# A three-branch decoder layer on one core: the passage from the projections to the first expert, rearranged

## The reference

```
# 1: recurrent attention (8 heads of 64)
b = (q * k).sum(-1) * SCALE;  a = -softplus(x @ W_alpha.T + bias).sum(-1)
ln = logaddexp(a_t + ln, b_t)
nm, sg = log-magnitude and sign of  sg*exp(a_t + nm) + sign(v_t)*exp(b_t + log(|v_t| + EPS))
y_t = sum over heads of sg * exp(nm - ln);   attention = y @ W_o.T
# 2: eight experts, gated by token
h = relu(x @ proj_in[e].T);  o = h @ proj_out[e].T
gate[b, s, e] = sum over k of weights[b, k, s] * (ensembles[b, k, s] == e)
# 3: gated ternary feed-forward net, three layers of 1024
x = layernorm(x + branch)          # after each of the three
```

## Time and profile before

| | us |
|---|---|
| median of 3 executions | 833.45 (833.44 to 836.83) |
| the profiled execution | 834.23 |
| its span, first to last instruction | 832.4 |
| TensorE busy | 791.9 (95%) |
| VectorE busy | 460.7 (55%) |
| ScalarE busy | 308.4 (37%) |
| GpSimd busy | 99.2 (12%) |
| mean granted TensorE clock | 0.985 of 2.4 GHz |

### The profile page before, as it was taken

The page is one execution under the profiler, slowest core; times in us unless marked ns, Lnnn a source line. Parts: engine busy times, 40 slices in busy tenths (PEclk is TensorE's granted clock), DMA queues, the critical chain, the costliest instruction groups (busy, mean ns, idle before and its releaser), DMA issues.

```text
span 832.4 us, 12868 instructions
## 1 busy us (share of the span) xinstructions
PE 791.9 (95%) x4342; PEld 685.4 (82%) x4342; DVE 460.7 (55%) x1119; ACT 308.4 (37%) x552; POOL 99.2 (12%) x100
## 2 busy tenths in 40 slices
PE   5999849999999999999999989999999999999995
PEld 4888728888899998999899988888888888888884
DVE  4788657665577775777665655323632363245113
ACT  5677622222232313223232226342634354326331
POOL 2465520000220201102020000000000000000000
PEclk9999969999999999999999999999999999999998
DMA  8700000000311223131311000000000000000000
GB/s 265 254 0 2 0 2 2 0 2 26 102 51 41 90 57 94 51 101 38 95 46 51 26 10 1 1 0 1 25 0 0 0 25 0 0 7 19 1 1 26
DMA packets 16451, 31.46 MB, mean 38 GB/s; under 512 B 1680, under 2 KB 6160, under 8 KB 16400
## 3 DMA queue, kind: packets, MB, share of 16 engines
q1 hardware_dynamic: 16400, 30.82, 11.8%
HBM read 28.72 MB, written 2.10 MB: 37 GB/s over the span
## 4 chain that ended last, share of the span: by engine, by line
PE 44%; issue 44%; DVE 7%; ACT 2%; POOL 1%; DMA 1%; DVEq 0%; POOLq 0%; SPq 0%; ACTq 0%
PE bank L701 23%; PE bank L793 21%; DVE sp L954 1%; DMA wp_lo_f<-in_wproj 1%; DVE al L943 1%; DVE x_tok L1046 1%; DVE masked L919 1%; DVE vp L936 1%; DVE sgn L932 1%; POOL wx_lo_r L487 1%; DVE hx_lo L1069 1%; ACT sp L567 0%; ACT sp L574 0%; ACT hx_hi L614 0%; POOL rstd L514 0%
## 5 line engine op out<-in xcount | busy, mean ns | idle before, releaser
L614 ACT ACTIVATE hx_hi<-bank 128x512 fp32r<-128x512 f32 x128 | 76.7, 599 | 266.9 <-PE bank L701 266.8
L793 PE MATMUL bank<-wx_hi,hx_hi 128*128 128x256 f32 x512 | 144.8, 283 | 1.3 <-DVE x_tok L1076 0.9
L793 PE MATMUL bank<-wx_hi,hx_lo 128*128 128x256 f32 x512 | 144.9, 283 | 0.0
L793 PE MATMUL bank<-wx_lo_r,hx_hi 128*128 128x256 f32 x512 | 144.8, 283 | 0.0
L1069 DVE SCALAR_TENSOR_TENSOR hx_lo<-bank,hx_hi 128x512 fp32r<-128x512 f32 x128 | 88.0, 690 | 93.9 <-ACT hx_hi L614 90.3
L701 PE MATMUL bank<-xT_hi,wx_hi 128*128 128x512 f32 x256 | 103.5, 404 | 2.7 <-DVE hx_lo L1069 1.1
L793 PEld LDWEIGHTS bank<-wx_hi,hx_hi 128*128 128x128 f32 x512 | 97.8, 191 | 6.1 <-DVE x_tok L1076 1.1
L701 PE MATMUL bank<-xT_lo,wx_hi 128*128 128x512 f32 x256 | 102.0, 398 | 0.0
L793 PEld LDWEIGHTS bank<-wx_lo_r,hx_hi 128*128 128x128 f32 x512 | 97.8, 191 | 3.9
L701 PE MATMUL bank<-xT_hi,wx_lo_r 128*128 128x512 f32 x256 | 100.7, 393 | 0.0
L872 PE MATMUL bank<-ha_hi_r,wf_hi_r 128*128 128x512 f32 x256 | 100.0, 391 | 0.0
(11 more groups left out here) (140 smaller groups left out, 1326.1 us busy)
## 6 DMA issues: line engine op xcount, KB each, us to landing
stage<-in_wffn SPq DMA_DIRECT2D x44, 256.0 KB, 2.7
wx_lo_f<-in_wx SPq DMA_DIRECT2D x16, 512.0 KB, 4.6
xs_lo_f<-in_xT SPq DMA_DIRECT2D x4, 512.0 KB, 5.0
...
```

What stands on the lines that cost most here:

```text
L614: act.activation(hx_hi[:, place, c], bank[b][:, :], ACT.Relu).then_inc(s_relu_ok, 1)
L793: mm = pe.matmul(bank[2 + j % 2][:, 0:D], x_, w_, start=(c == 0 and i == 0), stop=(c == XC - 1 and i == 2))
```

## The change

All edits lie between the start of the projections and the first expert products, except six pairs of gates.

- TensorE makes the v products of a group behind its first sequence (in the first group behind the second), not behind its fourth. `take_v` and its halves move with them, into the same group.
- VectorE sums the softplus of the sequence before (`a_sum`), not of the present one.
- ctx and itok are loaded whole, behind the second group of x; the gates of a sequence are made a group later, and those of the last six sequences during the first three expert steps.
- The halves of expert 0's weights are made in the two middle groups, a quarter at a time; its DMA is issued earlier. The halves of W_o are made in the last group.
- The first four output products go ahead of the transposes of `a_tok` and `b_tok`; the last two output banks are 6 and 7 and not 4 and 5. The extremes are transposed after two more products, not four.
- Residual, statistics and means of the first group go ahead of the flag and the branch, on VectorE; the root is made beside the flag and the branch. The long path works them out again. A second root (`rstd_again`) is made behind the norm in either case, for the long path, and VectorE waits for it before the first step.
- GpSimd waits for the normed rows of group 0 before the low parts of expert 1's weights.
- Behind the last output product TensorE makes 36 products of the identity with itself (plain f32, 128 columns) that nothing reads, and only then waits for the normed rows.

```diff
+IDLE = 36
...
-        masked_late = at("masked_late", o_w + 81920, [6, S])
+        masked_late = at("masked_late", o_w + 81920, [10, S])
...
-        UBANK = [bank[i] for i in (1, 2, 4, 5)]
+        UBANK = [bank[i] for i in (1, 2, 6, 7)]
...
+            for g in range(G - 1):
+                b = slice(J * g + J, J * g + 2 * J)
+                sp_.wait_ge(s_x0T_in, 16 * g + 16)
+                sp_.dma_start(x0T[:, b], xT[:, b]).then_inc(s_x0T_in, 16)
+                if g == 0:
+                    sp_.dma_start(ctx_sb[:, :, :], ctx).then_inc(s_gate_in, 16)
+                    sp_.dma_start(itok_sb[:, :, :], itok).then_inc(s_gate_in, 16)
+                if g == 1:
+                    load_first(0)
...
-            for e in range(2):
-                for i, part in enumerate((IN, OUT)):
-                    sp_.dma_start(wx_raw[:, e, part], wx[e, :, part]).then_inc(wx_in[e][i], 16)
+            load_first(1)
...
-                    if j < DC and not first:
-                        low_v((g - 1) * DC + j, g - 1, j)
+                    at = j - (2 if first else 1)
+                    if 0 <= at < DC:
+                        low_v(g * DC + at, g, at)
+                    elif not first and not last:
+                        quarter = (g - 1) * 2 + j // 3
+                        pool.wait_ge(s_wxhi_ok, quarter + 1)
+                        a = bass.ds(quarter * (WX // 4), WX // 4)
+                        pool.tensor_tensor(wx_lo[:, 0, a], wx_raw[:, 0, a], wx_hi[:, 0, a].bitcast(F32), ALU.subtract).then_inc(s_wxlo_ok, 1)
-            low_v(G * DC - DC, G - 1, 0)
-            low_v(G * DC - 1, G - 1, 1)
...
-            pool.wait_ge(s_A_ok, 1)
-            expert_low(0, 0)
-
             def root(g):
-                pool.wait_ge(s_ve_ok, g + 1)
+                pool.wait_ge(s_ve_ok, g)
...
-            root(0)
+
+            pool.wait_ge(s_ve_first, 1)
+            pool.tensor_tensor(rstd[:, :], var_eps[:, :], neghalf[:, :], ALU.pow).then_inc(s_rstd_ok, 1)
+            pool.wait_ge(s_again, 1)
+            pool.tensor_tensor(rstd_again[:, :], var_eps[:, :], neghalf[:, :], ALU.pow).then_inc(s_again_ok, 1)
+            pool.wait_ge(s_xn_ok, J)
             expert_low(1, 1)
...
-                    if j < DC and not first:
-                        high_v((g - 1) * DC + j, g - 1, j)
+                    at = j - (2 if first else 1)
+                    if 0 <= at < DC:
+                        high_v(g * DC + at, g, at)
+                    elif not first and not last:
+
+                        for part in wx_in[0]:
+                            act.wait_ge(part, 16)
+                        a = bass.ds(((g - 1) * 2 + j // 3) * (WX // 4), WX // 4)
+                        act.activation(wx_hi[:, 0, a], wx_raw[:, 0, a], ACT.Copy).then_inc(s_wxhi_ok, 1)
+                    if j == 0 and last:
+                        act.wait_ge(s_wo_in, 16)
+                        act.activation(wo_hi[:, :, :], wo_raw[:, :, :], ACT.Copy).then_inc(s_wo_hi_ok, 1)
             groups_behind(act, project)
-            act.wait_ge(s_wo_in, 16)
-            act.activation(wo_hi[:, :, :], wo_raw[:, :, :], ACT.Copy).then_inc(s_wo_hi_ok, 1)
-            high_v(G * DC - DC, G - 1, 0)
...
-            expert_high(0, 0)
-
+
+            for t in range(J):
+                act.wait_ge(s_u_mm, t + 1)
+                act.activation(u_sb[:, t], UBANK[t % 4][:, 0:D], ACT.Copy).then_inc(s_u_out, 1)
             act.wait_ge(s_tab_d, 2)
             act.activation(decT[:, :], decT[:, :], ACT.Exp).then_inc(s_tab_exp, 1)
             act.activation(betT[:, :], betT[:, :], ACT.Exp).then_inc(s_tab_exp, 1)
-            high_v(G * DC - 1, G - 1, 1)
-            for t in range(B):
+            for t in range(J, B):
                 act.wait_ge(s_u_mm, t + 1)
                 act.activation(u_sb[:, t], UBANK[t % 4][:, 0:D], ACT.Copy).then_inc(s_u_out, 1)
             expert_high(1, 1)
...
+            def values(g):
 
                 pe.wait_ge(s_wp_lo_ok, 4)
+                pe.wait_ge(s_xs_lo_ok, g * J + J)
                 for o in range(DC):
                     pe.wait_ge(s_v_out, g * DC + o + 1)
                     a = slice(3 * HD + o * P, 3 * HD + o * P + P)
                     rows = slice(g * J, g * J + J)
                     product(bank[6 + o][:, :].rearrange("p (j s) -> p j s", j=J), [pair for c in range(DC) for pair in three(
                         wp_hi[:, c, a], wp_lo[:, c, a], xs_hi[:, rows, c], xs_lo[:, rows, c])], s_v_mm)
+
...
+                    if j == (0 if g else 1):
+                        values(g)
...
+            pe.wait_ge(s_q_out, B + 1)
+            pe.wait_ge(s_k_out, B + 1)
+            pe.wait_ge(s_v_out, G * DC + 2)
+            pe.wait_ge(s_wo_lo_ok, 1)
+            for t in range(J):
+                output(t)
             pe.wait_ge(s_sp_ok, B + 2)
             pe.transpose(bank[0][:, 0:P], a_tok[:, :, :].rearrange("p b h -> p (b h)"), ident[:, :]).then_inc(s_ba_T, 1)
             pe.wait_ge(s_b_red, B + 2)
             pe.transpose(bank[3][:, 0:P], b_tok[:, :, :].rearrange("p b h -> p (b h)"), ident[:, :]).then_inc(s_ba_T, 1)
-            pe.wait_ge(s_q_out, B + 2)
-            pe.wait_ge(s_k_out, B + 2)
-            pe.wait_ge(s_wo_lo_ok, 1)
-            for t in range(0, 2 * J):
+            for t in range(J, 2 * J):
                 output(t)
             pe.wait_ge(s_chain, 8)
             pe.transpose(bank[0][:, P:2 * P], BT[:, :], ident[:, :]).then_inc(s_B_T, 1)
-            for t in range(2 * J, 3 * J):
+            for t in range(2 * J, 2 * J + 2):
                 output(t)
             pe.wait_ge(s_extremes_ok, 1)
             for i in range(3):
                 mm = pe.transpose(bank[3][0:1, (i + 1) * P:(i + 1) * P + P], extremes[:, i:i + 1], ident[:, :])
             mm.then_inc(s_extremes_T, 1)
-            for t in range(3 * J, 4 * J):
+            for t in range(2 * J + 2, 4 * J):
                 output(t)
+
+            pe.wait_ge(s_c_ok, 1)
+            for _ in range(IDLE):
+                pe.matmul(bank[0][:, 0:P], ident[:, :], ident[:, :], start=True, stop=True)
             pe.wait_ge(s_u_out, B + 4)
...
+            def a_sum(t, r):
+                dve.wait_ge(s_ln_ok, t + 1)
+                dve.scalar_tensor_tensor(out=sp[:, r], in0=al[:, r], scalar=0.0, in1=sp[:, r], op0=ALU.max,
+                                         op1=ALU.add).then_inc(s_sp_sum, 1)
...
                     dve.tensor_tensor(al[:, r], bank[r * 3][:, :], bias_b[:, :], ALU.add).then_inc(s_al_out, 1)
                     if j > 0 or not first:
+                        a_sum(t - 1, 1 - r)
                         b_sum(t - 1, 1 - r)
-                    if j == 0:
-                        dve.wait_ge(s_gate_in, 32 * g + 32)
-                    if j < J - 1 or not last:
+                    if j == 0 and not first:
+                        dve.wait_ge(s_gate_in, 32)
+                    if not first and (j < 2 or not last):
                         for e in range(2):
-                            gate(t, e, masked[:, e])
-                    if j < DC and not first:
-                        take_v((g - 1) * DC + j, j)
...
+                            gate(t - J, e, masked[:, e])
+                    if j == 2 and last:
+                        dve.wait_ge(s_wo_hi_ok, 1)
+                        dve.tensor_tensor(wo_lo[:, :, :], wo_raw[:, :, :], wo_hi[:, :, :].bitcast(F32), ALU.subtract).then_inc(s_wo_lo_ok, 1)
+                    at = j - (2 if first else 1)
+                    if 0 <= at < DC:
+                        take_v(g * DC + at, at)
             dve.sem_inc(s_vlo_ok, 2)
             groups_behind(dve, project)
-            take_v(G * DC - DC, 0)
+            a_sum(B - 1, 1)
             b_sum(B - 1, 1)
-            dve.wait_ge(s_wo_hi_ok, 1)
-            dve.tensor_tensor(wo_lo[:, :, :], wo_raw[:, :, :], wo_hi[:, :, :].bitcast(F32), ALU.subtract).then_inc(s_wo_lo_ok, 1)
...
+            def norm_means(n0, stats, means, var):
...
+            def residual(g, j, added, stats):
...
-            take_v(G * DC - 1, 1)
-            for e in range(2):
-                gate(B - 1, e, masked[:, e])
             dve.wait_ge(s_tab_exp, 2)
...
             dve.tensor_reduce(c_tok[:, :], bank[0][:, P:2 * P].rearrange("p (b h) -> p b h", h=H), AX_X, ALU.add).then_inc(s_c_ok, 1)
+            dve.wait_ge(s_c_ok, 1)
+            dve.wait_ge(s_xtok_in, 16)
+
+            for j in range(J):
+                residual(0, j, s_res_ok, s_bn_ok)
+            norm_means(0, s_bn_ok, s_mv_ok, s_ve_first)
             dve.wait_ge(s_extremes_T, 1)
             rows = bank[3][0:1, P:4 * P].rearrange("o (i n) -> o i n", i=3)
             dve.tensor_reduce(extreme[0:1, 0:2], rows[:, 0:2], AX_X, ALU.max)
...
-            dve.wait_ge(s_c_ok, 1)
 
 
             stepwise = dve.value_load(flag[0:1, 0:1], min_val=0, max_val=1)
             with dve.If(stepwise > 0):
                 step_path(dve)
-                dve.nop()
```

(20 more changed lines are left out.)

84 lines of the change are left out of this document (42 added, 42 removed).

## The result

| | before | after |
|---|---|---|
| median, us (11 executions each) | 836.21 (832.55 to 838.24) | 831.06 (829.12 to 831.97) |
| the profiled execution, its span | 834.23, 832.4 | 829.40, 827.6 |
| mean granted TensorE clock | 0.985 | 0.993 |

The ratio is 0.9939, 95% interval 0.9927 to 0.9951: 5.1 us less (4.1 to 6.1) where 9.8 were forecast. The sign was right, the size lies outside the range. The median before, 833.45 over three executions, is 836.2 over eleven.

A forecast was written before the change was run, and what follows sets the result against it. The prediction took TensorE to bound the projections and VectorE's chain to keep it waiting between projections and expert products. 7.7 + 2.1 = 9.8 us off the median 833.45 gave 823.6 us, range 819.5 to 828.5.

The forecast's parts named there:

- P to the first expert product: From the last projection product to the first expert product: the latter at 114.2 us instead of 121.94, 7.7 us less.
- clock behind it, to the first relu of step 1: First expert products, up to the fifth expert bank: full instead of half TensorE clock there, 2.1 us less.
- The step that failed: Projections: the same 336 matmuls, so TensorE through at 88.3 us as before, no change in time.
- Twelve gates at nothing: First three expert steps: twelve moved gates of 0.3 us cost nothing on an engine with slack, up to 3.6 us if not.
- 8.2 us for the 36 products: Behind the last output product: 36 unread f32 products at 0.23 us each, from 103.6 to 111.8 us.
- 2.4 us for four turned tiles: Between the unread products and the first expert product: four ready tile pairs are turned in 2.4 us, from 111.8 to 114.2.
- GpSimd's wait: At norm_apply: GpSimd waits for the normed rows, so norm_apply takes 1.38 us instead of 5.17.
- the early products: Rival at the unread products: 0.13 us each, over at 108.3 before the first normed row; 822.2 us, chance 0.24.
- the weights: Rival in the projections: expert 0's weight halves not covered by TensorE, up to 5 us; 830.8 us, chance 0.10.
- the slower case: Rival at the unread products: they become the path at half clock, first expert product at 126.1; 837.6 us, chance 0.06.
- the first rival: Products over early, VectorE decides; GpSimd's low parts hold up the next group's residuals by 0.9 us; 822.2 us, chance 0.24.
- The dip: Rival in the passage ahead of the expert products: a half clock in 97 to 104 us; 825.4 us, chance 0.18.

The follow-up runs named there:

- e1: Changed kernel with the low halves of the next x made ahead of q times k in the middle two projection groups; 827.28 us, ratio to before 0.9890.
- e9: Changed kernel with the v products of the two middle groups a turn later, behind their second sequence; 831.58 us (one execution).
- e5: Changed kernel with the gates of the last six sequences back in the last projection group; 833.93 us, ratio to before 0.9982.
- e12: e7 with late gates spread: one pair a step in the first three expert steps, three pairs in the fourth; 826.06 us, ratio to before 0.9876.
- e14: e1 plus 48 semaphore increments starting VectorE's program, late gates behind norm_apply, and 19 or 16 unread products; 822.19 or 822.65 us.
- e8: Changed kernel with residual, statistics and means of the first group behind the branch again; 830.82 us, ratio to before 0.9940.
- e10: Changed kernel with GpSimd's low parts of expert 1 behind the first root again, not waiting for the normed rows; 832.38 us (one execution).
- e4: Kernel before with one edit: GpSimd waits for the first group's normed rows before the low parts of expert 1; 833.37 us, ratio 0.9956.
- e2: Changed kernel with 28 unread products instead of 36; 829.56 us, ratio to before 0.9922.
- e3: Changed kernel with no unread products; 831.0 us, ratio to before 0.9927.
- e7: e1 and e2 together: low halves of x first and 28 unread products; 825.83 us, ratio to before 0.9889.

## Why the prediction was wrong

The sum of terms, in distances that do not depend on the start:

| term | forecast | measured |
|---|---|---|
| projections, from the 101st product to the last | 0 | +3.3 |
| P to the first expert product | -7.7 (114.2 for 121.94) | -8.25 (25.26 for 33.51) |
| clock behind it, to the first relu of step 1 | -2.1 | -2.24 |
| late gates | 0 | +1.0 |
| sum | -9.8 | -6.2 |
| the whole | | -5.1 (-6.1 to -4.1) |

- **The step that failed** is "the projections are the same 336 matmuls, so TensorE should be through at 88.3". I had looked at what moved off TensorE, at VectorE and at ScalarE, but not at what the moved v products themselves wait for. The list of edits held it: `values` waits for all four low halves, and the place of the fourth in GpSimd's turn is in the same listing. It cost 3.3 us; e1 removes it whole, and in e9 the stall goes where the v products were moved back. The signal I had named for it, a last projection later than 89 us, did come (89.78), but a start 1.6 us faster than before's hid that much of it: P is 1.7 us later. b_tok at 94.35 instead of 92.3 and the transpose of BT at 98.83 instead of 97.35 are mostly this shift (b_tok is 0.3 us late besides, BT 0.3 early): c_tok starts 9.63 us behind P, where the forecast has 10.0.
- **Twelve gates at nothing** cost 1.0 us (e5: gone without them). The bound of 3.6 held it. "An engine with slack" was true of the step and false of the place ahead of norm_apply (e12, e14).
- **Right:** 8.2 us for the 36 products (measured 8.04), though the transposes would have given 4.7; 2.4 us for four turned tiles (2.31); norm_apply 1.38; the full clock behind the products, 2.24 for 2.1. Weights and W_o in the projections cost nothing that e1 did not remove. By the Trainium skill's "FP8 and Floating Point Precision", section "TensorE Precision Notes", a true FP32 product is four passes; the trace agrees, 0.223 us for 128 columns beside 0.23 for 512 of the split types.
- **Right in sum, wrong in parts:** since the products set the end of the passage, the residual ahead of the branch was worth nothing (e8), and GpSimd's wait nothing (e10), though alone on the kernel before it is worth 3.1 us (e4). What the changed kernel needed was only a first normed row before P + 22.9, where the products end; the tables without take_v and gates (c_tok 2.6 us nearer to P) and the extremes two output products earlier gave that. How much each of these two gave is open.
- **Rivals:** the early products, the weights and the slower case fall (0.223 us a product, in after and e2). The residuals that the first rival has GpSimd hold up start at 118.44 us in after, its low parts end at 116.40, so they never met; nor does norm_apply read two tiles, as written there, but one. Two slips in the rivals' sums (as much again is 0.46 us a product, not 0.43; 48 x 0.09 is 4.3, not 4.5) touch neither forecast nor range. The dip did not come in the passage. It came elsewhere, though: at the entry of the feed-forward net behind a 2.4 us idle, half the clock for 3.4 us. The profiled execution before had been spared it, behind an idle of 2.5 us:

```profile
498.00:502.00 4.00, 3.79 (x17) 1.00 0.02 6
```

```profile
492.00:496.00 4.00, 4.00 (x12) 0.57 0.01 2
```

  e4, whose code there is the kernel's before, had the dip too (granted clock 0.50 from 500 to 502 us), and so did e1, e2 and e3; e7 and e8 did not. From the last relu of the expert pairs to the end of the span it is 344.7 us in before and 344.6 in e8, 346.2 in e4 and 346.5 in after. With this and the shortest jump of all (18.23 against 20.53 in e4) the profiled execution before was a lucky one: 834.23 where eleven have a median of 836.2. I took my sum against it and the median of three; against 836.2 the same -9.8 is 826.4, still 4.7 too low.
- **The two profiled executions** close without a rest: -6.2 from the terms, -1.6 from the start, +1.2 at the jump and +1.8 behind the expert pairs (the clock, half there in after and full in before) give -4.8, the difference of their spans.
- **Open:** 1.1 us (0.1 to 2.1) between the -6.2 of the terms and the -5.1 of the medians. Start, jump and the entry of the feed-forward net vary by 2 to 3 us each from one execution to the next, and one profile of each kernel can't tell whether the change moved their means.
